# A routed layer on one core: its indirect transfers issued in fours, with a wait for each four

## The chip, the cores and the metric

The kernel runs on one core of a Trainium2 chip. That core has five engines that run side by side, each with its own stream of instructions: PE (TensorE, matrix products), DVE (VectorE), ACT (ScalarE), POOL (GpSimd) and SP (SyncE, which here only starts transfers). They meet at semaphores: counters that an instruction or a landed transfer raises and that another engine's instruction waits for. The metric is the device time of one execution, in microseconds; the kernel before takes 627.26 us, the median of 3 runs (627.03 to 627.95).

## The reference, cut to what matters

The input x is 128 graphs of 64 rows of 128 numbers, 8192 rows in all. Two blocks are added to it in turn. The first is a graph step; the second sends each row to two of eight experts.

```
x = x + gnn(layernorm(x))     # h = layer_norm(.); relu((adj @ h) @ W_rel + b_rel + h @ W_root)
x = x + ffn(layernorm(x))
# ffn: gate = x @ Wg.T + bg; top 2 of 8 experts per row, softmax of the two scores
#      out += weight[e] * (relu(x @ W1[e].T + b1[e]) @ W2[e].T + b2[e])   for both experts
```

## The kernel before, in words

The 8192 rows are held in on-chip memory (tile X) as 64 tiles of 128 rows, and are worked on in four quarters q = 0 to 3 of 16 tiles. Every quarter goes through five steps.

1. Graph step, normalization and gate scores (PE, ACT, DVE).
2. Routing on DVE: `route_first`, `route_second`, `route_slots`, `route_rows` give each row two slots, sorted by expert and padded to blocks of 256. The slots are written to IDX (line L515), which raises `slots_made`.
3. `scatter(q)` on POOL: 32 indirect transfers (L298), each of 128 rows of 512 bytes, take the rows from the tile XHL to their slots in a DRAM buffer `rows[q]`. Each raises `scattered[q]` by 16 when it has landed.
4. The expert blocks: 24 blocks (`SB` = 6 per pass, 4 passes per quarter). SP loads three blocks at a time from `rows[q]` into XB (L237). PE turns them (L859), DVE copies them into XT (L535), PE forms the hidden values (L872, L876), ACT and DVE split them into HH and HL (L726, L540), PE forms the output (L893), ACT copies it into YB (L732), and SP stores three blocks at a time into the DRAM buffer `yrows[q]` (L262), which raises `y_out`. A quarter thus has eight stores.
5. `gather(q)` on POOL: 32 indirect transfers (L311) of 128 rows of 512 bytes bring each row's two results from `yrows[q]` into the tile YG. Eight of them raise one of the four semaphores `gathered[q][0..3]`. DVE then adds them into X with their weights (`combine`, L550), and SP writes X out (L270).

The order of it is fixed by hand, engine by engine. Quarters 0 and 1 do step 1 and 2 at the start. The graph step of quarters 2 and 3 is woven into the blocks of quarters 0 and 1, and their routing into the first pass of the blocks of quarters 1 and 2: `slots_made` for quarter 2 comes in the middle of the first pass of quarter 1's blocks, that for quarter 3 in the first pass of quarter 2's blocks. Additions woven into the blocks are those of two quarters earlier: `combine` of quarter 0 runs beside quarter 2's blocks, that of quarter 1 beside quarter 3's. Before DVE enters quarter 2 or quarter 3 it waits for all four semaphores of that gather:

```
if not graph:                      # q = 2 and q = 3
    for i in range(NG):
        dve.wait_ge(gathered[q - 2][i], 2 * GT * 16)
```

The additions of quarters 2 and 3 come after the last block. SP waits for `scattered[0]` before the first load of rows, and for `scattered[q + 1]` before the first load of the next quarter.

POOL has one queue, run in order: scatter(0), scatter(1), scatter(2), gather(0), scatter(3), gather(1), gather(2), gather(3). scatter(q) begins by waiting for `slots_made`, gather(q) for the last `y_out` of its quarter. Between the transfers of one of these eight stretches POOL waits for nothing.

Of the kernel before, what the change touches and what calls it, by code (L numbers as in the profile page):

```python
# [18 lines left out]
GT = 4  # L36
# [23 lines left out]
def build(nc, x, adj, wrel, wroot, wg, w1, w2, b1, b2, kf, kh, out):  # L60
    ctx = ExitStack()
    with ctx:
# [6 lines left out]
        def sem(name):  # L69
            return ctx.enter_context(nc.semaphore(name))  # L70
# [108 lines left out]
        scattered = [sem(f"scattered{q}") for q in range(Q)]  # L179
# [10 lines left out]
        gathered = [[sem(f"gathered{q}_{i}") for i in range(NG)] for q in range(Q)]  # L190
# [83 lines left out]
        @block.gpsimd  # L274
        def _(pool):
            nc.gpsimd.memset(ADJ[:, :], 0.0).then_inc(adj_zero, 1)
            nc.gpsimd.memset(ZERO, 0.0).then_inc(zero_made, 1)
            nc.gpsimd.memset(B1[:, :], 0.0).then_inc(bias_zero, 1)
            nc.gpsimd.memset(B2[:, :], 0.0).then_inc(bias_zero, 1)

            for n, (w, s) in enumerate(((YG[0], W1S), (YG[1], W2S))):
                pool.wait_ge((w1_in, w2_in)[n], 16)
                nc.gpsimd.tensor_scalar(w[:, :], w[:, :], s, 1.0, ALU.mult, ALU.mult).then_inc(scaled, 1)
            for n, (w, hi, lo) in enumerate(((YG[0], W1H, W1L), (YG[1], W2H, W2L))):
                pool.wait_ge(whi_made, n + 1)
                nc.gpsimd.tensor_tensor(lo[:, :], w[:, :], hi[:, :], ALU.subtract).then_inc(wlo_made, 1)

            def scatter(q):  # L290
                pool.wait_ge(slots_made, q + 1)
                pool.wait_ge(xlo_made, (q + 1) * NG)
                pool.wait_ge(zero_out[q], 16)
                for t in range(TQ):
                    for k in range(2):
                        col = (q * 2 + k) * TQ + t
                        src = (q % 2 * TQ + t) * 2 * P
                        nc.gpsimd.indirect_dma_start(  # L298
                            rows[q], bass.IndirectOffsetOnAxis(ap=IDX[:, col:col + 1], axis=0),
                            XHL[:, src:src + 2 * P].bitcast(F32), None).then_inc(scattered[q], 16)  # L300

            def gather(q):
                for j in range(2):
                    pool.wait_ge(y_out[j], 16 + (q + 1) * 16 * NG)
                if q >= 2:
                    pool.wait_ge(combined, (q - 1) * NG)
                for t in range(TQ):
                    for k in range(2):
                        col = (q * 2 + k) * TQ + t
                        dst = (t * 2 + k) * P  # L310
                        nc.gpsimd.indirect_dma_start(  # L311
                            YG[q % 2][:, dst:dst + P], None, yrows[q],
                            bass.IndirectOffsetOnAxis(ap=IDX[:, col:col + 1], axis=0)).then_inc(gathered[q][t // GT], 16)

            scatter(0)
            scatter(1)
            scatter(2)
            gather(0)
            scatter(3)
            gather(1)  # L320
            gather(2)
            gather(3)
            for q in range(Q):
                for i in range(NG):
                    pool.wait_ge(gathered[q][i], 2 * GT * 16)
# [684 lines left out]
```

## Time and profile before

| | |
|---|---|
| median of 3 runs | 627.26 us (627.03 to 627.95) |
| profiled execution, span from first to last instruction | 878.1 us |
| mean granted TensorE clock in it | 0.761 of full speed |
| busy: PE, PE weight loads, DVE, POOL, ACT | 471.1, 395.1, 385.6, 272.6, 237.7 us |
| indirect transfers on POOL | 128 of L298 (123.2 us busy), 128 of L311 (121.3 us busy) |

For the profiled execution no time of its own is recorded beside this span. It is 250.8 us longer than the median of the runs, so its stretches can't be added up to the measured time as they stand. An engine counts as busy while it runs a compute instruction or, on POOL, prepares the descriptors of an indirect transfer; the movement of the data comes after that and is not in the busy time. In the rows of the 40 slices each digit is the busy share of 22 us in tenths.

### The profile page before, as it was taken

The page shows a single profiled execution, that of the slowest core. Times are in us where ns is not written, and L with a number is a line of the kernel's source. Part 1 is how long each engine was busy: PE and PEld are TensorE (multiplying, and loading weights), DVE is VectorE, ACT ScalarE, POOL GpSimd, SP SyncE. Part 2 cuts the span into 40 slices and gives each one's busy share as a digit, 9 for nine tenths or more (in the row PEclk, how much of TensorE's full clock was granted, in tenths as well). Part 3 has the DMA queues.
Part 4 walks back from the last instruction along what each step waited for, and adds up shares of the span by engine and source line. Part 5 has one row for each costly group of instructions (what it writes and reads, how often), then busy time and mean ns, then how long its engine had stood idle before and what let it go on. Part 6 is the DMA issues. An engine that isn't in the chain of part 4 may idle for free.

```text
span 878.1 us, 14976 instructions
## 1 busy us (share of the span) xinstructions
PE 471.1 (54%) x4776; PEld 395.1 (45%) x4777; DVE 385.6 (44%) x1146; ACT 237.7 (27%) x467; POOL 272.6 (31%) x268
## 2 busy tenths in 40 slices
PE   0613243441799997401099997201299951899500
PEld 0613233330688886201088886100188840688400
DVE  2979933830454667200044668000055620456622
ACT  0413100210356554000056553000044410344200
POOL 3053373067000000777400001777300067000274
PEclk9955575565799999655589999655599975899955
DMA  9980012011112112211112112111122222221341
GB/s 346 416 287 1 19 51 64 6 58 51 43 44 78 56 57 67 68 54 51 33 44 78 57 57 82 52 54 51 27 73 72 72 78 53 74 73 54 135 132 57
DMA packets 32173, 70.78 MB, mean 81 GB/s; under 512 B 14458, under 2 KB 14714, under 8 KB 31364
## 3 DMA queue, kind: packets, MB, share of 16 engines
q1 hardware_dynamic: 21520, 37.66, 13.0%
q0 software_dynamic: 8192, 16.79, 6.6%
q10 hardware_dynamic: 2420, 15.77, 4.4%
q8 instruction: 27, 0.44, 0.2%
q14 instruction: 14, 0.11, 0.0%
HBM read 32.45 MB, written 37.75 MB: 80 GB/s over the span
## 4 chain that ended last, share of the span: by engine, by line
PE 42%; issue 20%; another core or an unknown queue 13%; DVE 13%; DMA 4%; ACT 3%; POOL 3%; SPq 2%; ACTq 0%; DVEq 0%; POOLq 0%
PE PH L876 14%; PE PY L893 13%; PE PH L872 5%; POOL YG L311 3%; DMA ADJ<-in_adj 3%; PE PX L859 2%; ACT N L695 1%; PE PY L886 1%; SPq L223 1%; ACT N L677 1%; PE PA L824 1%; DVE VARN L377 1%; DVE MDIF L376 1%; DVE N L442 1%
## 5 line engine op out<-in xcount | busy, mean ns | idle before, releaser
L298 POOL DMA_INDIRECT rows<-XHL,IDX x128 | 123.2, 962 | 347.1 <-DVE IDX L515 309.3
L540 DVE SCALAR_TENSOR_TENSOR HL<-PH,HH 128x512 f16<-128x512 f32 x192 | 129.8, 689 | 207.0 <-ACT HH L726 114.1
L726 ACT ACTIVATE HH<-PH 128x512 f16<-128x512 f32 x192 | 113.6, 596 | 263.1 <-PE PH L876 107.9
L311 POOL DMA_INDIRECT YG<-yrows,IDX x128 | 121.3, 948 | 202.7 <-DMA yrows<-YB 164.3
L876 PE MATMUL PH<-XT,W1H 128*128 128x256 f16 x768 | 144.3, 281 | 22.8 <-issue 22.6
L893 PE MATMUL PY<-W2H,HL 128*128 x768 | 131.0, 223 | 31.8 <-issue 31.8
L893 PE MATMUL PY<-W2H,HH 128*128 x768 | 131.1, 223 | 25.3 <-issue 25.3
L893 PE MATMUL PY<-W2L,HH 128*128 x768 | 109.3, 223 | 42.1 <-issue 42.1
L535 DVE COPY XT<-PX 128x512 f16<-128x512 f16 x96 | 40.5, 422 | 168.6 <-issue 63.1
L876 PE MATMUL PH<-XT,W1L 128*128 128x256 f16 x384 | 107.8, 281 | 12.3 <-issue 12.3
L876 PEld LDWEIGHTS PH<-XT,W1H 128*128 x768 | 76.3, 100 | 55.8 <-issue 32.9
L893 PEld LDWEIGHTS PY<-W2H,HL 128*128 128x128 f16 x768 | 76.4, 99 | 34.1 <-issue 32.7
L893 PEld LDWEIGHTS PY<-W2H,HH 128*128 128x128 f16 x768 | 76.4, 100 | 29.0 <-issue 27.8
L872 PE MATMUL PH<-KH,B 128*128 128x512 f16 x192 | 76.0, 396 | 19.3 <-issue 17.0
L732 ACT ACTIVATE YB<-PY 128x256 f32<-128x256 f32 x96 | 36.7, 382 | 163.1 <-remote 91.2
L893 PEld LDWEIGHTS PY<-W2L,HH 128*128 128x128 f16 x768 | 60.4, 99 | 44.7 <-issue 44.7
L859 PE MATMUL PX<-KH,XB 128*128 128x128 f16 x384 | 39.8, 225 | 31.8 <-issue 19.6
L550 DVE SCALAR_TENSOR_TENSOR X<-YG,PR,X 128x128 f32<-128x128 f32 (+1 forms) x128 | 36.1, 346 | 31.3 <-DMA YG<-yrows,IDX 31.0
L876 PEld LDWEIGHTS PH<-XT,W1L 128*128 x384 | 38.6, 100 | 18.7 <-issue 13.6
L859 PEld LDWEIGHTS PX<-KH,XB 128*128 128x128 f16 x384 | 27.3, 102 | 36.1 <-issue 30.2
L872 PEld LDWEIGHTS PH<-KH,B 128*128 x192 | 19.1, 99 | 26.8 <-issue 24.7
L886 PE MATMUL PY<-B,KH 128*128 x96 | 26.9, 280 | 0.8 <-issue 0.7
(154 smaller groups left out, 559.8 us busy)
## 6 DMA issues: line engine op xcount, KB each, us to landing
rows<-XB ACTq DMA_DIRECT2D x4, 3072.0 KB, 29.8
XB<-rows SPq DMA_DIRECT2D x32, 384.0 KB
yrows<-YB SPq DMA_DIRECT2D x32, 384.0 KB, 2.3
out<-X SPq DMA_DIRECT2D x16, 256.0 KB
X<-in_x SPq DMA_DIRECT2D x3, 1024.0 KB, 28.2
YG<-in_w ACTq DMA_DIRECT2D x1, 2048.0 KB, 9.6
ADJ<-in_adj SPq DMA_DIRECT2D x32, 64.0 KB, 3.8
YG<-in_w SPq DMA_DIRECT2D x1, 2048.0 KB, 29.7
```

The source lines that it names most:

```text
L298: nc.gpsimd.indirect_dma_start(rows[q], bass.IndirectOffsetOnAxis(ap=IDX[:, col:col + 1], axis=0), XHL[:, src:src + 2 * P].bitcast(F32), N ...
L311: nc.gpsimd.indirect_dma_start(YG[q % 2][:, dst:dst + P], None, yrows[q], bass.IndirectOffsetOnAxis(ap=IDX[:, col:col + 1], axis=0)).then_ ...
L535: nc.vector.tensor_copy(XT[:, j % 2 * 2 * BW:(j % 2 + 1) * 2 * BW], PX[:, 0:BW].bitcast(F16)).then_inc(xT_made[j], 1)
L540: nc.vector.scalar_tensor_tensor(HL[:, at:at + 2 * BW], PH[h][:, :], 0.0, HH[:, at:at + 2 * BW], ALU.max, ALU.subtract).then_inc((loa_made ...
L550: ins = nc.vector.scalar_tensor_tensor(xv, y, cols(PR, (q * 2 + e) * TQ + i * GT + k, 1), xv, ALU.mult, ALU.add)
L726: nc.scalar.activation(HH[:, at:at + 2 * BW], PH[h][:, :], ACT.Relu).then_inc((hia_made, hib_made)[h][j], 1)
L732: nc.scalar.mul(YB[:, j * BW:(j + 1) * BW], PY[j % 2][:, 0:BW], 1.0 / YS).then_inc(y_made[j], 1)
L859: last = nc.tensor.transpose(px[:, s * BW + t * P:s * BW + (t + 1) * P], src[:, s * P:(s + 1) * P], ident16)
L872: nc.tensor.matmul(ph[:, :], cols(B1, e, P), KH[:, H_B1M + h * 2 * BW:H_B1M + (h + 1) * 2 * BW], start=True, stop=False, skip_group_check= ...
L876: last = nc.tensor.matmul(ph[:, c % 2 * BW:(c % 2 + 1) * BW], cols(w, e * C + c * P, P), v, start=False, stop=(c % 2 == 1 and w is W1L), s ...
L886: nc.tensor.matmul(py[:, 0:BW], KH[:, H_B2M:H_B2M + P], cols(B2, e, P).unsqueeze(1).to_broadcast([P, 2, P]), start=True, stop=False, skip_ ...
L893: last = nc.tensor.matmul(py[:, t * P:(t + 1) * P], h[:, at:at + P], cols(w, e * C + c * P, P), start=False, stop=(c == C - 1 and w is W2L ...
```

## The change

After every two tiles, that is after every four indirect transfers, POOL waits until these four (and so all before them of that stretch) have landed. It does so in all four scatters and all four gathers. Nothing else is changed; the lines of the changed file stand 17 lower from the top because empty lines at its head are gone.

```
@@ scatter(q)
                         nc.gpsimd.indirect_dma_start(
                             rows[q], bass.IndirectOffsetOnAxis(ap=IDX[:, col:col + 1], axis=0),
                             XHL[:, src:src + 2 * P].bitcast(F32), None).then_inc(scattered[q], 16)
+                    if t % 2 == 1:
+                        pool.wait_ge(scattered[q], (t + 1) * 32)
@@ gather(q)
                         nc.gpsimd.indirect_dma_start(
                             YG[q % 2][:, dst:dst + P], None, yrows[q],
                             bass.IndirectOffsetOnAxis(ap=IDX[:, col:col + 1], axis=0)).then_inc(gathered[q][t // GT], 16)
+                    if t % 2 == 1:
+                        pool.wait_ge(gathered[q][t // GT], (t % GT + 1) * 32)
```

POOL's instructions before, from scatter(2) to gather(1) (L298 is the scatter, L311 the gather; a wait stands in brackets on the instruction that carries it):

```order
19 L298 DMA rows<-XHL,IDX 6144x128 [waits zero_out2,xlo_made,slots_made]
20 L298 DMA rows<-XHL,IDX 6144x128 x31
21 L311 DMA YG<-yrows,IDX 128x128 [waits y_out1,y_out0]
22 L311 DMA YG<-yrows,IDX 128x128 x31
23 L298 DMA rows<-XHL,IDX 6144x128 [waits zero_out3,xlo_made,slots_made]
24 L298 DMA rows<-XHL,IDX 6144x128 x31
25 L311 DMA YG<-yrows,IDX 128x128 [waits y_out1,y_out0]
```

The same queue now, from the last fours of scatter(2) into gather(0) (L281 is the scatter, L296 the gather):

```order
59 L281 DMA rows<-XHL,IDX 6144x128 [waits scattered2]
60 L281 DMA rows<-XHL,IDX 6144x128 x3
61 L281 DMA rows<-XHL,IDX 6144x128 [waits scattered2]
62 L281 DMA rows<-XHL,IDX 6144x128 x3
63 L296 DMA YG<-yrows,IDX 128x128 [waits y_out1,y_out0,scattered2]
64 L296 DMA YG<-yrows,IDX 128x128 x3
65 L296 DMA YG<-yrows,IDX 128x128 [waits gathered0_0]
66 L296 DMA YG<-yrows,IDX 128x128 x3
67 L296 DMA YG<-yrows,IDX 128x128 [waits gathered0_0]
```

The order of the transfers is the same. A stretch of 32 now holds seven waits inside it, each carried by the first transfer of the next four, and the wait for its last four is carried by the first instruction of the stretch that follows.

## Rows read from the trace of the kernel before

**Rows 1.** The page's 40 slices of the span: PE and POOL.

```profile
PE   0613243441799997401099997201299951899500
POOL 3053373067000000777400001777300067000274
```

**Rows 2.** One stretch (columns: PE, PEld, DVE, ACT, POOL busy; PEclk; DMA share; GB/s).

```profile
349.00:440.00 91.00, 16.66 (x92) 9.65 (x93) 8.77 (x33) 5.43 (x13) 60.86 (x64) 0.54 0.17 51
```

**Rows 3.** DVE in time at the start: start us, us, what [idle before <-releaser].

```profile
122.58 0.33 DVE L391 TENSOR_SCALAR SC<-SCI 128x16 f32<-128x16 f32 x1 [1.90 <-remote]
...
146.56 0.69 DVE L417 TENSOR_TENSOR TMP<-PH,KF 128x512 f32<-128x512 f32 x1 [23.64 <-remote]
...
181.25 0.42 DVE L535 COPY XT<-PX 128x512 f16<-128x512 f16 x1
```

**Rows 4.** The page's transfers: KB each, median us to landing.

```profile
yrows<-YB SPq DMA_DIRECT2D x32, 384.0 KB, 2.3
```

**Rows 5.** SP's stores of three blocks each, in time.

```profile
236.81 0.38 SPq L262 DMA_DIRECT2D yrows<-YB  x1
...
346.80 0.36 SPq L262 DMA_DIRECT2D yrows<-YB  x1
...
447.42 0.36 SPq L262 DMA_DIRECT2D yrows<-YB  x1
...
489.05 0.36 SPq L262 DMA_DIRECT2D yrows<-YB  x1
...
502.18 0.35 SPq L262 DMA_DIRECT2D yrows<-YB  x1
...
542.51 0.36 SPq L262 DMA_DIRECT2D yrows<-YB  x1
...
637.35 0.36 SPq L262 DMA_DIRECT2D yrows<-YB  x1
...
691.71 0.35 SPq L262 DMA_DIRECT2D yrows<-YB  x1
...
702.62 0.35 SPq L262 DMA_DIRECT2D yrows<-YB  x1
...
751.59 0.36 SPq L262 DMA_DIRECT2D yrows<-YB  x1
```

**Rows 6.** DVE where it enters quarters 2 and 3.

```profile
525.35 0.41 DVE L535 COPY XT<-PX 128x512 f16<-128x512 f16 x1
...
697.31 0.69 DVE L540 SCALAR_TENSOR_TENSOR HL<-PH,HH 128x512 f16<-128x512 f32 x1 [0.18 <-ACT HH L726]
...
700.52 0.69 DVE L540 SCALAR_TENSOR_TENSOR HL<-PH,HH 128x512 f16<-128x512 f32 x1 [1.55 <-ACT HH L726]
```

**Rows 7.** Quarter 2's slots on DVE, and POOL's 64 issues: first, last.

```profile
348.62 0.19 DVE L515 SCALAR_TENSOR_TENSOR IDX<-SLA,SLB 128x32 int32<-128x32 int32 x1
...
349.09 0.96 POOL L298 DMA_INDIRECT rows<-XHL,IDX  x1 [128.86 <-DVE IDX L515]
...
428.21 0.94 POOL L311 DMA_INDIRECT YG<-yrows,IDX  x1 [0.30 <-issue]
```

**Rows 8.** Quarter 3's slots on DVE.

```profile
543.43 0.19 DVE L515 SCALAR_TENSOR_TENSOR IDX<-SLA,SLB 128x32 int32<-128x32 int32 x1
```

**Rows 9.** scatter(0)'s last issue on POOL, and SP's load that waits for it.

```profile
140.90 0.96 POOL L298 DMA_INDIRECT rows<-XHL,IDX  x1 [0.30 <-issue]
...
143.15 0.82 SPq L237 DMA_DIRECT2D XB<-rows  x2
```

**Rows 10.** The tail: two issues of gather(3), and the additions that wait for them.

```profile
837.10 0.95 POOL L311 DMA_INDIRECT YG<-yrows,IDX  x1 [0.30 <-issue]
...
840.23 2.32 DVE L550 SCALAR_TENSOR_TENSOR X<-YG,PR,X 128x128 f32<-128x128 f32 x8 [8.46 <-DMA YG<-yrows,IDX]
...
867.19 0.94 POOL L311 DMA_INDIRECT YG<-yrows,IDX  x1 [0.30 <-issue]
...
869.75 2.31 DVE L550 SCALAR_TENSOR_TENSOR X<-YG,PR,X 128x128 f32<-128x128 f32 x8 [7.67 <-DMA YG<-yrows,IDX]
```

More of the change, by code:

```diff
@@ L300, in scatter @@
                             XHL[:, src:src + 2 * P].bitcast(F32), None).then_inc(scattered[q], 16)
+                    if t % 2 == 1:
+                        pool.wait_ge(scattered[q], (t + 1) * 32)
             def gather(q):
@@ L313, in gather @@
                             bass.IndirectOffsetOnAxis(ap=IDX[:, col:col + 1], axis=0)).then_inc(gathered[q][t // GT], 16)
+                    if t % 2 == 1:
+                        pool.wait_ge(gathered[q][t // GT], (t % GT + 1) * 32)
             scatter(0)
```

## The prediction, made before the changed kernel had run

> **What bounds the kernel now.** I read the 40 slices of the page first [rows 1]. The reader is to see two things there: in the middle of the program PE is busy nine tenths of most slices, so PE's matrix products set the pace, and it falls to nearly nothing in just those slices in which POOL is at 7. POOL's work (the indirect transfers) and the other engines' work exclude each other in this execution, although nothing in the program makes them. The sums over one such stretch say it in numbers: in 91 us PE is busy 16.66 us and DVE 8.77 us, at half or slightly over half the clock, while POOL issues its 64 transfers without a pause [rows 2].
>
> Is that so in the timed runs too? I worked that out from how much time it takes. In the start DVE stands idle twice, 1.9 and 23.6 us, for something remote [rows 3]: 25.5 us. From DVE's first copy of a turned block (181.25) to the first store of quarter 0 (236.81) it takes 55.6 us [rows 3, 5]; the same piece of quarter 2 takes 542.51 - 525.35 = 17.2 us [rows 5, 6], so 38.4 us are lost. From the first to the second store of quarter 1 there are 447.42 - 346.80 = 100.6 us, where an undisturbed half pass of that quarter takes 502.18 - 489.05 = 13.1 [rows 5]: 87.5 us. The same in quarter 2: 637.35 - 542.51 = 94.8 against 702.62 - 691.71 = 10.9: 83.9 us. And 751.59 - 702.62 = 49.0 against 10.9: 38.1 us. The sum is 273.4 us, and 878.1 - 273.4 = 604.7 us. The median of the runs is 627.26 us. So the timed runs can hold at most some 23 us of such stretches, and I take it that they belong to the profiled execution and that in the timed ones PE goes on beside POOL. The page has no time of that execution beyond its span, so I make the sum on a timeline from which these five stretches are cut out.
>
> On that timeline there is a wait that the profile hides. Quarter 3's slots are ready at 543.43 + 0.19 = 543.62 [rows 8]. DVE enters quarter 3 when it has done its last half of quarter 2, at 697.31 + 0.69 = 698.0 [rows 6], and there it wants the whole of gather(1). Without the stretch, that is 698.0 - 637.35 = 60.65, plus one half pass of 10.9, less the 1.1 us by which the slots come after the store at 542.51: 70.5 us. POOL needs longer for scatter(3) and gather(1). The like pair before it took from the slots at 348.81 to the end of the last issue at 429.15, which is 80.3 us for 64 issues [rows 7], and 1.6 us until the last has landed (below): 81.9 us. So DVE waits 81.9 - 70.5 = 11.4 us there already, and the timeline gives 604.7 + 11.4 = 616.1 us. The 11.2 us missing to 627.26 I put down to what lies around the span and to what I can't see.
>
> For quarter 2 it is different: slots at 348.81, entry at 525.35 [rows 6, 7]. That is 525.35 - 447.42 = 77.9, plus 13.1, less 348.81 - 346.80 = 2.0: 89.0 us against 81.9. Gather(0) is in time by 7.1 us.
>
> The end is bound by POOL alone: from the last store on, gather(3) issues 32 transfers while all other engines but DVE's short additions stand still.
>
> **What one wait costs.** Before, the pause between two issues is 0.30 us. Now the first of the next four starts only when the last of the four has landed and POOL has woken.
> - Gather: the last issue of all ends at 867.19 + 0.94 = 868.13, and the addition that waits for it starts at 869.75 [rows 10]: 1.62 us. POOL's own start after a semaphore is 349.09 - 348.81 = 0.28 us [rows 7]. One wait adds 1.62 + 0.28 - 0.30 = 1.60 us.
> - Scatter: its last issue ends at 141.86, and SP, which waits for it, starts its load at 143.15 [rows 9]: 1.29 us. One wait adds 1.29 + 0.28 - 0.30 = 1.27 us.
> The lower end for both is 1.29 - 0.30 = 0.99, if the waiter's own wake-up is already inside these figures. The upper end is the landing beside heavy traffic: the eighth issue of the tail ends at 838.05 and its addition starts at 840.23 [rows 10], 2.18 us, so 2.16 us per wait. I take the middle figures, as they are the rows of just this landing.
>
> The Trainium skill, DMA: Bandwidth & Descriptors, section "Anatomy of one DMA — SWDGE (gpsimd) path", gives about 2.0 us plus the bytes over 436e3 for one transfer, that is an estimate of 2.15 us for 64 KB, and says that a write into HBM has the slowest receipt. Rows 10 give 2.56 us from start to landing for a gather, longer than that, and rows 9 give 2.25 us for the scatter into DRAM, the shorter of the two, against the rule. By the rule a wait would add 2.15 - 0.94 - 0.02 = 1.2 us in either, and the sum below would come to 35 us instead of 45. The rows decide.
>
> **The change part by part.**
> - A scatter has eight waits before the next stretch may begin: 8 x 1.27 = 10.2 us. A gather has seven before its own last landing: 7 x 1.60 = 11.2 us. A pair of both takes 81.9 + 21.4 = 103.3 us.
> - scatter(0): SP's first load waits for it, now 7 x 1.27 = 8.9 us later. The load was issued at 143.15; with 0.4 us for the issue, 2.3 us for landing (a store of the same 384 KB [rows 4]) and 0.6 us to turn the block the rows would be ready at 155.3 us instead of 146.4. DVE would take them at 181.25 - 25.5 = 155.7 [rows 3]. Just hidden, by its routing of quarter 1: 0 us; with 2.16 per wait it is 6 us, and less cover if more of DVE's start was slow than its two idle rows show.
> - scatter(1): its slots come after scatter(0) or with its end, and quarter 1's blocks come a whole quarter (eight half passes, over 80 us) later: 0 us.
> - Entry into quarter 2: 103.3 - 89.0 = 14.3 us of new wait on DVE. Queued behind it are the copies into XT and the low halves, for which PE waits. The rows behind the entry of quarter 3 show DVE idle 1.55 us for ACT [rows 6], so about 1.5 us of a wait would be swallowed: 12.8 us. What was late before was nothing; now it is POOL.
> - Entry into quarter 3: the wait of 11.4 us becomes 103.3 - 70.5 = 32.8 us: 21.4 us more, in full, as the swallowed part is already used.
> - gather(2): it starts at quarter 3's entry and ends within 40 + 12 us, while quarter 3's blocks take over 80: 0 us.
> - Tail, gather(3): 7 x 1.60 = 11.2 us. The eighth landing was waited for before too. DVE's additions of a group (2.3 us) go beside the next fours, as now.
> Sum: 12.8 + 21.4 + 11.2 = 45.4 us, and 627.26 + 45.4 = 672.7 us.
>
> With 0.99 us per wait: 14.9 us on a pair, so 14.9 - 7.1 - 1.5 = 6.3, then 14.9, then 6.9: 28.1 us, 655 us. With 2.16: 32.4 on a pair, so 23.8, 32.4, 15.1 and 6 at the start: 77 us, 705 us. All waits at the upper end is improbable, since three of the four such landings in the tail took 1.6 us, as the last one did.
>
> **The rivals.**
> 1. POOL is quicker in the timed runs, where nothing is recorded of it. With 1.0 us per issue in place of 1.25 a pair takes 66 us before and 87 us after: quarter 2 is entered without a wait (89.0), quarter 3 with 87 - 70.5 = 16.5, new in full, and the tail adds 11.2: 28 us, 655 us. For it: the other engines are plainly slower in the profiled execution. Against: the timeline then misses 30 us instead of 11, as the wait of 11.4 and 8 us of the tail are gone.
> 2. Only the tail pays. If the timed runs too held some 20 us of the slow stretches, DVE would come later to both entries and the pairs would have more cover; to hide 21.4 at both it takes 33 us of delay in quarter 2, more than the 23 us that the median leaves. Partly so it is possible: tail 11.2 us alone, 638.5 us.
> 3. Faster: the pauses give the others room. The engines crawl when POOL issues without a pause, and if the 11.2 us that I can't place, and the 11.4 us put down to the wait, are such crawling (22.6 us in all), fours with pauses could end it. The slow stretch of 64 issues ends some 10 us after the last of them, about 1.4 us per transfer, and fours take (4 x 1.26 + 1.27) / 4 = 1.58 us per transfer, so no backlog would form. The gain of 22.6 less the tail's 11.2 gives 615.9 us, if the entries stay hidden. It decides only where each wait costs less than 22.6 / 7 = 3.2 us, which it does, and where POOL's pairs fit before the entries, which by the rows they don't.
> 4. The waits cost 2.16 us each: 705 us, worked out above.
>
> **How the numbers follow.** Forecast with waits near 1.3 to 1.6 us and both entries late: 0.60, own range 660 to 688. Rival 1: 0.18. Rival 2: 0.10. Rival 3: 0.04. Rival 4: 0.05. The rest, 0.03, is no change. The likeliest is 672.7 us. The range, 648 to 694 us, takes in rival 1 and the lower bound of the cost of a wait, and leaves out rivals 2 to 4. A measurement of this kernel tells about 0.2% from no change: faster 0.04, same 0.03, slower 0.93.
>
> **What would show it.** In the profile of the changed kernel every fourth pause on POOL is about 1.6 us (scatter) or 1.9 us (gather) instead of 0.30, and a stretch of 32 takes 49 to 52 us instead of 40. At the entries of quarters 2 and 3 DVE stands idle before its copy into XT until the last gather has landed, about 13 and 33 us. The last store to the end is 11 us longer. The slow stretches of the profiled execution should shrink or go, so its span may well get shorter while the timed runs get longer. I am wrong if the timed kernel is not slower by at least the tail's 7 us; wrong in the second step if DVE doesn't wait at the two entries; wrong in the first if a pause on POOL is under 1.2 or over 2.5 us.

## The result, and the profile after

The changed kernel takes 685.31 us (median of 4 runs, 682.0 to 686.08) against 627.14 us of the kernel before (4 runs, 626.38 to 627.95): 58.2 us or 9% slower, ratio 1.0902 with a 95% interval of 1.0855 to 1.0948. The forecast was 672.7 us, with a range of 648 to 694.

The profiled execution after is no longer than the timed ones: its span is 683.6 us, and that same execution took 685.36 us. So the time of an execution is its span plus 1.8 us, profiled or not. The 40 slices of the page, 17 us each, are the counterpart of [rows 1]:

```profile
PE   0640409316999999889999737999910899991000
...
POOL 5008315656550000065555622555556564103562
```

PE stays at 8 and 9 where POOL is at 5 and 6. The exclusion of [rows 1, 2] is gone. What stands out instead are two drops of PE, to 3 and to 0, at the ends of POOL's two long stretches. They are DVE's waits. DVE in order of time, with the idle time before the instruction and what ended it (the counterpart of [rows 3, 6]):

```profile
156.94 0.42 DVE L522 COPY XT<-PX 128x512 f16<-128x512 f16 x1 [6.03 <-PE PX L846]
...
385.95 0.18 DVE L441 TENSOR_TENSOR LG<-PA,KF 128x32 f32 x1
401.71 0.42 DVE L522 COPY XT<-PX 128x512 f16<-128x512 f16 x1 [15.57 <-DMA YG<-yrows,IDX]
...
531.85 0.42 DVE L522 COPY XT<-PX 128x512 f16<-128x512 f16 x1 [37.44 <-DMA YG<-yrows,IDX]
```

The first row is the start: 6.0 us of waiting for the first rows. The last two are the entries into quarters 2 and 3: 15.57 and 37.44 us until the last gather had landed. The slots of quarters 2 and 3 (the counterpart of [rows 7, 8]):

```profile
290.70 0.19 DVE L502 SCALAR_TENSOR_TENSOR IDX<-SLA,SLB 128x32 int32<-128x32 int32 x1
...
421.31 0.19 DVE L502 SCALAR_TENSOR_TENSOR IDX<-SLA,SLB 128x32 int32<-128x32 int32 x1
```

From the slots to DVE's copy behind the entry it takes 401.71 - 290.89 = 110.8 us and 531.85 - 421.50 = 110.4 us; that is the length of a pair of scatter and gather with its waits. Of POOL's fifteen pauses with a wait in quarter 2's pair, four:

```profile
297.95 0.96 POOL L281 DMA_INDIRECT rows<-XHL,IDX  x1 [1.55 <-DMA rows<-XHL,IDX]
...
327.36 0.95 POOL L281 DMA_INDIRECT rows<-XHL,IDX  x1 [3.17 <-DMA rows<-XHL,IDX]
...
355.24 0.95 POOL L296 DMA_INDIRECT YG<-yrows,IDX  x1 [3.56 <-DMA YG<-yrows,IDX]
...
361.66 0.95 POOL L296 DMA_INDIRECT YG<-yrows,IDX  x1 [1.73 <-DMA YG<-yrows,IDX]
```

Most pauses are 1.5 to 1.6 us in a scatter and 1.7 to 1.8 in a gather. Four of the fifteen here are 2.8 to 3.7 us, and three of the next pair's are 2.8 to 4.3. Six of these seven begin 0.7 to 1.5 us after SP has started a load of three blocks (384 KB), itself just behind a store of the same size. The pause of 3.17 us, for instance, begins at 327.36 - 3.17 = 324.19:

```profile
322.83 0.34 SPq L220 DMA_DIRECT2D XB<-rows  x1
```

All fifteen pauses sum to 31.6 us in this pair and 31.7 us in the next, against 4.5 us before. SP's stores show where the quarters grew (the counterpart of [rows 5]):

```profile
178.98 0.38 SPq L245 DMA_DIRECT2D yrows<-YB  x1
...
389.18 0.35 SPq L245 DMA_DIRECT2D yrows<-YB  x1
...
420.70 0.36 SPq L245 DMA_DIRECT2D yrows<-YB  x1
...
434.67 0.36 SPq L245 DMA_DIRECT2D yrows<-YB  x1
...
499.05 0.35 SPq L245 DMA_DIRECT2D yrows<-YB  x1
...
546.45 0.36 SPq L245 DMA_DIRECT2D yrows<-YB  x1
```

From the last store of quarter 1 to the first of quarter 2 it takes 31.5 us, from the last of quarter 2 to the first of quarter 3 47.4 us. The tail, now and in the trace before (the counterpart of [rows 10]):

```profile
622.01 0.94 POOL L296 DMA_INDIRECT YG<-yrows,IDX  x1 [37.40 <-DMA yrows<-YB]
```

```profile
828.17 1.00 POOL L311 DMA_INDIRECT YG<-yrows,IDX  x1 [82.65 <-DMA yrows<-YB]
```

From POOL's first issue of gather(3) to the end it is 683.6 - 622.0 = 61.6 us, in the trace before 878.1 - 828.2 = 49.9 us: 11.7 us more. The same piece without waits lies between 49.0 and 51.1 us in the other traces below, so a term read from one pair of traces is good to about 1 us.

### The profile page after: what moved, and what is told of

Same layout as the page of the kernel before. It is cut to its first block and busy times, and to the rows that moved or that the text cites. A ratio compares the mean times of both kernels' runs of the same rounds, so it can differ in the third digit from the quotient of the medians.

```text
span 683.6 us, 14981 instructions
## 1 busy us (share of the span) xinstructions
PE 437.6 (64%) x4776; PEld 383.5 (56%) x4777; DVE 385.6 (56%) x1146; ACT 237.5 (35%) x467; POOL 276.2 (40%) x268
## 5 line engine op out<-in xcount | busy, mean ns | idle before, releaser
L281 POOL DMA_INDIRECT rows<-XHL,IDX x128 | 126.9, 991 | 220.6 <-DVE IDX L502 113.5
L296 POOL DMA_INDIRECT YG<-yrows,IDX x128 | 121.3, 948 | 130.9 <-DMA YG<-yrows,IDX 60.8
L863 PE MATMUL PH<-XT,W1H 128*128 128x256 f16 x768 | 141.5, 280 | 0.0
L880 PE MATMUL PY<-W2H,HH 128*128 x768 | 128.4, 221 | 0.0
L880 PE MATMUL PY<-W2H,HL 128*128 x768 | 128.2, 221 | 0.0
L880 PE MATMUL PY<-W2L,HH 128*128 x768 | 106.3, 220 | 0.0
L859 PE MATMUL PH<-KH,B 128*128 128x512 f16 x192 | 75.4, 393 | 12.2 <-issue 9.0
L846 PE MATMUL PX<-KH,XB 128*128 128x128 f16 x384 | 38.0, 223 | 65.0 <-DVE XT L522 52.6
L859 PEld LDWEIGHTS PH<-KH,B 128*128 x192 | 18.9, 98 | 20.1 <-issue 17.5
L818 PE MATMUL PA<-KF,N 128*128 128x128 f32 x8 | 2.2, 435 | 38.7 <-DVE N L429 38.7
```

Source lines behind the costliest of these rows:

```text
L281: nc.gpsimd.indirect_dma_start(rows[q], bass.IndirectOffsetOnAxis(ap=IDX[:, col:col + 1], axis=0), XHL[:, src:src + 2 * P].bitcast(F32), N ...
L296: nc.gpsimd.indirect_dma_start(YG[q % 2][:, dst:dst + P], None, yrows[q], bass.IndirectOffsetOnAxis(ap=IDX[:, col:col + 1], axis=0)).then_ ...
L818: last = nc.tensor.transpose(tile(bank, t), tile(N4, k * GT + t), ident)
L846: last = nc.tensor.transpose(px[:, s * BW + t * P:s * BW + (t + 1) * P], src[:, s * P:(s + 1) * P], ident16)
L859: nc.tensor.matmul(ph[:, :], cols(B1, e, P), KH[:, H_B1M + h * 2 * BW:H_B1M + (h + 1) * 2 * BW], start=True, stop=False, skip_group_check= ...
L863: last = nc.tensor.matmul(ph[:, c % 2 * BW:(c % 2 + 1) * BW], cols(w, e * C + c * P, P), v, start=False, stop=(c % 2 == 1 and w is W1L), s ...
```

## Experiments

Theory A is that of the prediction: a wait costs what it adds on the path that sets the end, nothing under cover. Theory B is that POOL's pauses cost the same wherever they are. Two more came up on the way: C, on some chips the other engines crawl while POOL issues long stretches, and fours prevent it; D, that crawl comes with any transfers of POOL. All kernels are derived from the changed one or from the kernel before; `scatter` and `gather` below are its two loops on POOL. Every run stands beside runs of the kernel before on its own chip, and that matters here. Of each edit only the lines that matter are shown.

**Waits in one stretch at a time.** Four kernels, run together:

```
# e1: waits in gather(3) only             e2: in scatter(2) and gather(0) only
# e3: in scatter(3) and gather(1) only    e4: in scatter(0) only
-                    if t % 2 == 1:
+                    if q == 3 and t % 2 == 1:      # e1; the others accordingly
```

> Waits in fours in gather(3) alone, all other stretches as before. Theory A (a wait costs what it adds on the path that sets the end, and nothing under cover): the tail grows by 11.7 us, as in the trace of the changed kernel (from POOL's first issue to the end 61.6 us against 49.9): 627.1 + 11.7 = 638.8 us. Theory B (pauses on POOL cost the same everywhere, 58.2 us over some 60 waits, about 0.97 us each): 634 us.

> Waits in fours in scatter(2) and gather(0) alone. Theory A: DVE reaches quarter 2 some 95 us after its slots (trace of the changed kernel: 290.9 to 386.1), the pair took 81.9 us and takes about 110 us with waits; DVE waits 15.6 us there, and 14 to 15.6 of it are new: 641 to 643 us. Theory B (equal cost everywhere): 15 waits, 641.7 us. The two can't be told apart here, but with the other three runs.

> Waits in fours in scatter(3) and gather(1) alone. Theory A: DVE reaches quarter 3 72.9 us after its slots; the pair took 81.9 us, so DVE waited 9 us before; with waits it waits 37.4 us: 28 us more, 655 us. Theory A without the hidden wait (POOL quicker in the timed runs, in time at quarter 3 before): up to 37 us more, 664 us. Theory B: 15 waits, 642 us.

> Waits in fours in scatter(0) alone. Theory A with the cover of the trace after: DVE stands idle 6.0 us for the first rows, which it did not before: 633 us. As predicted before the result (hidden): 627 us. Theory B: 7 waits, 634 us.

On this chip the kernel before took 885.05 us (7 runs, 880.78 to 887.9) and not 627. All four expectations were therefore numbers for another case, and only the differences can be read:

| waits in | us | against 885.05 | ratio, 95% interval |
|---|---|---|---|
| gather(3) | 897.20 | +12.2 | 1.0136 (1.0093 to 1.018) |
| scatter(2), gather(0) | 827.51 | -57.5 | 0.9375 (0.932 to 0.9429) |
| scatter(3), gather(1) | 834.26 | -50.8 | 0.9425 (0.9382 to 0.9468) |
| scatter(0) | 857.30 | -27.8 | 0.9685 (0.9644 to 0.9726) |

The tail came out as expected by A (11.7), since there POOL alone works, and against B, which has 7. The other three became faster, which neither theory had. The slices of e2, 20.6 us each:

```profile
PE   0532351544199999788777972111999813999400
...
POOL 4035076027500000065555027774000373000373
```

Where POOL issues in fours (the long row of 5s) PE is at 7 and 8; in POOL's other stretches (7s) it falls to 1 and 2, much as in [rows 1]. So the slow stretches of the first trace are no matter of profiling: they are in the timed runs of this chip, and the waits remove them where they are put. A look at how such a stretch begins, in the trace of the kernel before, PE (POOL issues from 349.09 on without a pause):

```profile
357.04 0.27 PE L876 MATMUL PH<-XT,W1L 128*128 128x256 f16 x1
...
359.01 0.27 PE L876 MATMUL PH<-XT,W1L 128*128 128x256 f16 x1 [1.15 <-issue]
...
366.79 0.37 PE L876 MATMUL PH<-XT,W1H 128*128 128x256 f16 x1 [0.33 <-issue]
...
396.89 1.12 PE L831 MATMUL PB<-KF,N 128*128 128x128 f32 x4 [28.32 <-issue]
```

For some 8 us, six to seven transfers, PE goes on as ever. Then a matrix product comes every 1.4 us, with nothing that it waits for in the trace, and at last there is a gap of 28 us. A product itself takes 0.27 to 0.38 us there, about what it took just before, so it is not the clock: the time goes between the products.

**Where the crawl is absent.** The next four ran on a chip where the kernel before took 629.04 us (17 runs, 625.4 to 631.61).

```
# e5: no waits; gather(1) issues its first 16 transfers only, DVE and POOL wait for those only;
#     half of quarter 1's expert results is left out
+                        if q == 1 and t >= TQ // 2:
+                            continue
```

> The kernel before, but gather(1) issues only its first 16 transfers and DVE waits for those alone at quarter 3; the second half of quarter 1's expert results is left out (old contents of the tile are added). 16 issues of 1.25 us, 20 us, go from POOL before quarter 3. Theory A (DVE waits some 9 us at quarter 3 in the timed runs of the kernel before): 627.1 - 9 = 618 us. If POOL is in time there (no wait before): 627 us.

Measured: 621.58 us, 7.5 us less (ratio 0.9865, 0.9818 to 0.9912). The hidden wait at quarter 3 is there, near the size that A gives. The edit also takes the traffic of 16 transfers away, and this run alone does not separate the two; the spans do it roughly, below. This trace is also the undisturbed one that the prediction lacked. Its stores, its slots of quarter 3 and DVE's last work before the entry:

```profile
178.57 0.38 SPq L245 DMA_DIRECT2D yrows<-YB  x1
...
389.67 0.35 SPq L245 DMA_DIRECT2D yrows<-YB  x1
...
405.23 0.36 SPq L245 DMA_DIRECT2D yrows<-YB  x1
...
419.14 0.36 SPq L245 DMA_DIRECT2D yrows<-YB  x1
...
483.45 0.35 SPq L245 DMA_DIRECT2D yrows<-YB  x1
...
493.83 0.36 SPq L245 DMA_DIRECT2D yrows<-YB  x1
```

```profile
406.14 0.19 DVE L502 SCALAR_TENSOR_TENSOR IDX<-SLA,SLB 128x32 int32<-128x32 int32 x1
...
478.12 0.69 DVE L527 SCALAR_TENSOR_TENSOR HL<-PH,HH 128x512 f16<-128x512 f32 x1 [0.18 <-ACT HH L715]
```

From the last store of quarter 1 to the first of quarter 2 15.6 us (after the change 31.5), from the last of quarter 2 to the first of quarter 3 10.4 us (47.4). DVE enters quarter 3 at 478.81, 72.5 us behind the slots at 406.33, where the prediction had 70.5. The pair without waits takes 81.9 us, so by this estimate 9.4 us of waiting is what this kernel took away.

```
# e6: no waits, POOL's order changed      e7: the same order, with the waits in fours
             scatter(1)
+            gather(0)
             scatter(2)
-            gather(0)
+            gather(1)
             scatter(3)
-            gather(1)
```

> The kernel before with POOL's order changed: gather(0) ahead of scatter(2), gather(1) ahead of scatter(3); no waits added. The results to gather are there 12 to 17 us before the slots of the next quarter, so gather(1) is done about 40 us earlier. Theory A: the hidden wait at quarter 3 goes: 618 us. If there is no such wait: 627 us.

> The changed kernel (waits in fours everywhere) with gather(0) ahead of scatter(2) and gather(1) ahead of scatter(3). Theory A: DVE's waits at quarters 2 and 3 go, as each gather then ends about 52 us after its quarter; the rows of the next quarter must be there by its first load: at quarter 3 the pair ends some 97 us after the results are there, 12 to 15 us beyond the quarter's own 83 us, so a wait of SP of up to 15 us can take their place. The start and the tail stay: 618 + 6 + 11.7 = 636 us, up to 651 with SP's wait. Theory B (equal cost for each wait): 618 + 58 = 676 us.

e6 took 628.92 us (ratio 0.999, 0.9963 to 1.0018): nothing gained, a miss. e7 took 677.35 us, where A had 636 to 651: a miss too, and B's 676 fits. The waits say why. PE in e6 and in e7:

```profile
PE PX L842 <- DMA XB<-rows: 3.5, 1, 3.5
```

```profile
PE PX L846 <- DMA XB<-rows: 49.9, 3, 27.8
```

In e7 no entry waits for a gather any more; PE waits for the rows that scatter brings instead, 49.9 us in three waits (one of them the start's). The scatter is now the later one of the pair, and its deadline is harder than I had written: SP must load the first three blocks of the next quarter while the last three of this one are at work, some 10 us ahead of DVE's entry, and SP's store of finished blocks stands behind that wait. In e6 this shows in SP's stores at the end of quarter 2:

```profile
463.92 0.35 SPq L245 DMA_DIRECT2D yrows<-YB  x1
...
477.20 0.42 SPq L245 DMA_DIRECT2D yrows<-YB  x1
...
490.70 0.35 SPq L245 DMA_DIRECT2D yrows<-YB  x1
```

They come 13.3 and 13.5 us apart, in e5 10.1 and 10.9: 5.7 us lost, most of the 7.5 that should have been gained. In e7 two such store intervals are 24.3 and 37.6 us long where the same two are 14.2 and 10.1 in e5, together 37.6 us more. So B's agreement is by chance: the cost sits in waits with a name, not in each pause.

```
# e8: waits after every eight transfers
-                    if t % 2 == 1:
+                    if t % 4 == 3:
```

> Waits after every eight transfers in all stretches, half as many. Theory A: per pair +14 instead of +28 us: quarter 2 in time or just so (96 against 95): 0 to 1; quarter 3 +14; tail 3 waits x 1.6 = +5; start +1 to 2: 648 us. Theory B: half of 58.2: 656 us. Its profile tells from how many transfers in a row the other engines slow down in a profiled execution.

646.43 us (ratio 1.0276, 1.0235 to 1.0317), +17.4. A had 648, B 656. DVE's waits at the entries:

```profile
DVE XT L522 <- DMA YG<-yrows,IDX: 21.5, 1, 21.5
```

One wait of 21.5 us is left, at quarter 3, and none at quarter 2. Half the pauses cost less than a third of the time: cover, as A says, and against B.

**The changed kernel where the crawl is, and two better orders.** On a third chip the kernel before took 884.51 us (15 runs, 879.94 to 888.23).

```
# e10: waits after every eight, none in gather(3), and      e11: no waits, and
+            gather(1, first 8 transfers)
             scatter(3)
-            gather(1)
+            gather(1, the other 24)
```

> The changed kernel once more, beside the kernel before on the same chip. On a chip where the kernel before takes some 627 us: 685 us, 9% slower. On a chip where it takes some 885 us, theory C (there the other engines crawl once about ten transfers have been issued in a row, in timed runs too, and fours never let that begin): 685 us all the same, 23% faster. Rival D (the crawl belongs to the chip and returns with any transfers of POOL): above 850 us.

> Waits after every eight transfers, none in gather(3), and the first eight transfers of gather(1) ahead of scatter(3). Where the kernel before takes 627 us: eights gave 646.4; the tail's 3 waits (5 us) go, and DVE's wait at quarter 3 falls by about 10 us, as POOL no longer idles for 12 us before the slots: 631 us. Where it takes 885 us: theory C gives the same, some 631 to 650 us; if the crawl needs less than eight in a row, over 700 us.

> The kernel before with one move: the first eight transfers of gather(1) ahead of scatter(3), no waits. Where the kernel before takes 627 us: POOL's pair for quarter 3 ends about 10 us earlier, DVE's hidden wait of 8 to 9 us goes and scatter(3) still lands before SP's first load of quarter 3: 619 us. If the gain of 7.5 us in the half gather came from something else: 627 us. Where it takes 885 us: no change within 1%, as DVE comes late there.

e9, the changed kernel itself, took 714.57 us: 170 us or 19.5% faster than before (ratio 0.8055, 0.8018 to 0.8092). D is out. C holds in its sign but missed its 685 us by 30. Its slices:

```profile
PE   0640626618699999877778787877786887993000
...
POOL 4009126656520000055555500655554546002652
```

and PE's sums over quarter 2's pair, here and after the change on the first chip (columns as in [rows 2]):

```profile
305.00:410.00 105.00, 82.65 (x824) 68.95 (x823) 44.43 (x128) 44.60 (x99) 60.98 (x64) 0.92 0.28 85
```

```profile
291.00:400.00 109.00, 91.39 (x1035) 80.15 (x1035) 56.50 (x170) 55.58 (x121) 61.95 (x64) 0.95 0.30 93
```

824 products in 105 us against 1035 in 109 us: with fours PE does 83% as much per microsecond, and the second stretch even holds 14 us of DVE's wait at the entry. In exchange DVE waits little at the entries here, since it comes late:

```profile
DVE XT L522 <- DMA YG<-yrows,IDX: 7.6, 1, 7.6
```

On the first chip it waited 15.57 + 37.44 = 53.0 us at the two entries. So more of the crawl is left than the 30 us: an estimate from the two traces is 30 + 45 = 75 us, of which 45 take the place of waits.

e10 took 829.56 us (ratio 0.9349, 0.9312 to 0.9385): a miss, C had at most 650; the other branch of what was expected (over 700 if fewer than eight in a row start the crawl) is what came. Eight in a row are enough for most of the crawl; its slices:

```profile
PE   0523180555899997543479996444699954899400
...
POOL 4044266066100000666610005666300066000274
```

e11 took 879.17 us (ratio 0.9937, 0.9911 to 0.9963), within the 1% expected there.

**The last one.** e12 is e10's order with fours, on a chip where the kernel before took 627.81 us (10 runs).

```
# e12: waits after every four but none in gather(3); first 8 of gather(1) ahead of scatter(3)
-                    if t % 2 == 1:
+                    if q < 3 and t % 2 == 1:       # gather only
```

> The changed kernel (waits in fours) without the waits in gather(3), and with the first eight transfers of gather(1) ahead of scatter(3). Where the kernel before takes 627 us: 685 less the tail's 11.7 and less some 12 us of DVE's wait at quarter 3: 662 us, 5 to 6% slower than before. Where it takes 885 us: fours gave 714.6; less 12 for the tail (waits in the tail alone cost 12.2 there) and 0 to 5 at quarter 3, as the mild crawl covers most of that wait: 698 to 703 us, and the fastest of all kernels there.

659.56 us (ratio 1.0519, 1.0479 to 1.0558), 25.8 us less than the changed kernel. DVE's waits at both entries together:

```profile
DVE XT L523 <- DMA YG<-yrows,IDX: 34.7, 2, 24.2
```

34.7 us, the longer one 24.2 where it was 37.44, and nothing in the tail. The two terms aimed at gave 12.6 us in the tail (from POOL's first issue of gather(3) to the end 49.0 us instead of 61.6) and 13.2 us at quarter 3. The other wait is 10.5 us instead of 15.57 with no edit behind it, and the first store comes 2.7 us later: landings and the start vary that much between executions. No kernel here is shown to be faster than the kernel before both where the crawl is and where it is absent. For e11 the gain of some 8 us expected where it is absent is not shown: it ran only where the crawl is.

## Why the prediction was right, and where it was not

**The stretches in the trace.** This step failed, though the total did not suffer: "I take it that they belong to the profiled execution". They don't come with profiling. Timed runs of the kernel before took 885.05 and 884.51 us on two chips and 627 to 629 us on others, and executions with a profile took their span plus 1.8 us in both cases. So a span of 878.1 us goes with a time of some 880 us, and the profile of before and the times of before came from different conditions. Cutting the stretches out was right for the runs that were timed; the reason given was wrong, and the 0.93 given to a slower kernel holds only where the crawl is absent. Rival 3, "the pauses give the others room", to which I gave 0.04, is what happens where the crawl is: 19.5% faster. The size of its gain, 22.6 us, was read from the wrong runs.

**The cost of one wait.** Scatter 1.27 us expected, 1.53 - 0.30 = 1.23 measured; gather 1.60 expected, 1.77 - 0.30 = 1.47 measured. Both are right for a quiet landing. The fixed cost and rate that the Trainium skill gives (DMA: Bandwidth & Descriptors, "Anatomy of one DMA — SWDGE (gpsimd) path"), from which I had estimated 1.2 us for either, fit the scatter and are 0.3 us short for the gather. What the sum left out is the landing beside SP's loads and stores: four of fifteen pauses in one pair and three in the next take 2.8 to 4.3 us. The pauses of a pair grew by 31.6 - 4.5 = 27.1 us instead of 21.4; at the quiet prices they would have grown by 8 x 1.23 + 7 x 1.47 = 20.1. An upper figure for such a landing was in the text (2.16 us per wait) but had been read as improbable for all waits, because I looked at the tail, where only the first wait is disturbed.

**Term by term**, with e5 as the kernel without waits:

| term | predicted | measured |
|---|---|---|
| start, to the last store of quarter 1 | 0 | -0.5 (389.18 against 389.67; first store 178.98 against 178.57) |
| entry into quarter 2 | 12.8 | 15.9 (31.5 against 15.6) |
| entry into quarter 3 | 21.4 | 29.5 (47.4 less 10.4, less the hidden 7.5) |
| tail | 11.2 | 10.5 (61.6 against 620.2 - 569.1 = 51.1); 11.7 against the trace before |
| sum | 45.4 | 55.4, of 58.2 |

The two spans say the same: 683.6 - 620.2 = 63.4 us, less the hidden 7.5 is 55.9. The 2.3 us to 58.2 are within what the kernel before varies between the two chips (627.14 and 629.04) and e5's own interval (5.5 to 11.4 us for the 7.5). Without a hidden wait it would be 63.4, above the interval of the measured change (53.6 to 59.5).

- Start: DVE does wait 6.0 us for the first rows, but it is ready at 150.9 instead of 154.8 in e5, and the rest goes in the first blocks. That it cancels was luck, the mechanism was not foreseen. It does not cancel as well in every execution: the first store comes at 178.57 and 179.85 in the two traces here without waits in scatter(0), at 178.98, 181.07 and 181.64 in three with fours.
- Quarter 2: the cover was longer than the cut timeline gave, 386.14 - 290.89 = 95.3 us and not 89.0, as the half pass with the routing in it takes 19 to 20 us even undisturbed and I had cut it to 13.1. The longer pair (110.8 against 103.3) outweighs that, so part of this term's nearness is two errors that offset each other. The 1.5 us that I let the engines swallow were not swallowed: a wait of 15.6 us cost 15.9.
- Quarter 3: cover 72.9 us (predicted 70.5), pair 110.4 (103.3), wait 37.44 (32.8), before the change 9.4 (11.4). The step is right in kind, and mis-sized mainly by the landings beside SP's transfers: 29.5 us where the sum had 21.4, the largest miss of all terms.
- scatter(1) and gather(2) under cover: nothing in the stores of quarters 0 and 3 speaks against it (94.6 us from first to last store of quarter 0, in e5 94.4).

**Rivals.** 1 (POOL quicker in the timed runs) is out: the execution of 685.36 us shows the same 0.96 and 0.94 us per issue. 2 (only the tail pays) is out by the two entries. 4 lies nearer than I gave it: not every wait costs 2.16 us, but the mean of the fifteen is 1.8.

**What stays open.** It stays open what makes the other engines crawl on some chips when POOL issues without a pause, and why only there. The traces show PE with nothing to wait for; whether it lacks instructions or something else was not separated by any run. The load of the DMA engines does not look like the reason: their busy share is 0.17 in the slow stretch of [rows 2] and 0.30 in the changed kernel's pair, where PE keeps its pace (1001 products in the first 95 us of it, 995 in the same 95 us of e5). Nor is it shown that the crawl belongs to a chip and not to a moment: each of the two chips on which it was timed was used for one round of runs only.

## What to carry to other kernels

A wait for a landing in a queue costs its pause times the number of waits only where the queue's end is waited for, so find each consumer's deadline, subtract the chain that leads to it, and look for waits that exist already: at quarter 3 there was no cover left and every pause counted in full. Price the pause from landings beside the traffic that will be there, not from the quietest ones. And when the span of the profiled execution and the times differ by 40%, don't explain it away: ask for both on the same chip, because the change that costs 9% on one gained 19.5% on the other.

## What the runs showed of the hardware that was not expected

- The same program took 627 to 629 us on some chips and 884 to 885 us on two others, all its runs within 1% of each other on each. The difference lies in the stretches in which POOL issues indirect transfers of 64 KB one after another (1.26 us each): there PE slowed after some seven of them in quarter 2's pair (in the scatter of quarter 0 after ten). Waiting after four in each stretch brought the time on such a chip from 884.5 to 714.6 us, after eight (none in the last gather) to 829.6 us.
- An indirect transfer of 128 rows of 512 bytes lets POOL start again 1.53 us (into DRAM) or 1.77 us (into on-chip memory) after its issue has ended. Where SP had started a store and a load of 384 KB shortly before (the load 0.7 to 1.5 us before the pause in six cases of seven), it was 2.8 to 4.3 us.
